# Fetching half of the search stretches from SP instead of GpSimd in a graph attention kernel

## The reference

```python
h = x @ w_lin + b_lin                       # x: (12500, 64)
msg = h[edge_src]                           # 400,000 edges, sorted by edge_dst
counts = segment_sum(ones, edge_dst)        # edges of each node
pos = arange(e) - starts[edge_dst]
dense[edge_dst, pos] = msg                  # (12500, 32, 64), edges past the 32nd are dropped
mask[edge_dst, pos] = True
xb = mab(dense, dense, enc weights, mask)   # attention among a node's up to 32 messages
xp = relu(xb @ pma_lin_w + pma_lin_b)
p  = mab(seed, xp, pma weights, mask)       # one learned query per node
dd = mab(p, p, dec weights)
out = layernorm(x + relu(dd))
```

## Time and profile before

| | |
|---|---|
| Median of 3 runs | 4168.89 us |
| The profiled execution: time / span | 4176.05 / 4174.2 us |
| PE busy | 3126.7 us (75%) |
| DVE busy | 3035.1 us (73%) |
| POOL busy | 3067.2 us (73%) |
| ACT busy | 1659.8 us (40%) |
| DMA | 88 GB/s over the span |
| TensorE's granted clock | 0.912 of full speed, mean |

### The profile page before, as it was taken

How to read it: one execution, slowest core, us unless ns; L and a number is a source line. 1 busy time by engine, 2 the same in 40 slices (tenths; PEclk the granted TensorE clock), 3 DMA queues, 4 the chain that set the end, 5 groups by cost and what they waited for, 6 DMA issues and landing times.

```text
span 4174.2 us, 87208 instructions
## 1 busy us (share of the span) xinstructions
PE 3126.7 (75%) x30724; PEld 2000.1 (48%) x30724; DVE 3035.1 (73%) x7088; ACT 1659.8 (40%) x2990; POOL 3067.2 (73%) x3236
## 2 busy tenths in 40 slices
PE   5677777777777777777777777777777777777776
PEld 3444444454444444444444454444444444444444
DVE  4677777777777777777777777777776777777876
ACT  2343443444434434443444343443443444434443
POOL 3777777777777777777777777777777777777772
PEclk7898999999999999999999999999999999999998
DMA  5333333333333333333333333333333333333331
GB/s 197 87 85 88 85 88 84 87 88 85 87 86 87 85 88 85 87 85 88 85 87 86 87 85 88 85 87 85 88 87 85 88 85 87 85 88 85 97 95 35
DMA packets 170668, 368.55 MB, mean 88 GB/s; under 512 B 56190, under 2 KB 109094, under 8 KB 170230
## 3 DMA queue, kind: packets, MB, share of 16 engines
q0 software_dynamic: 158032, 342.73, 30.7%
q1 hardware_dynamic: 11877, 19.76, 1.3%
q10 hardware_dynamic: 320, 0.10, 0.0%
HBM read 349.58 MB, written 16.32 MB: 88 GB/s over the span
## 4 chain that ended last, share of the span: by engine, by line
POOL 63%; issue 21%; PE 7%; DMA 4%; DVE 3%; POOLq 1%; ACT 0%; SPq 0%; ACTq 0%; DVEq 0%
POOL gathered L547 61%; DMA gathered<-node_table,idx 4%; POOL windows L510 2%; PE ps L724 2%; PE ps L651 2%; PE ps L697 2%; DVE xb L1119 1%; PE ps L639 1%; DVE probs_diag L1193 0%; DVE flags L908 0%; POOLq L122 0%; PE ps L606 0%; POOLq L124 0%; PE ps L752 0%; DVE h L1075 0%
## 5 line engine op out<-in xcount | busy, mean ns | idle before, releaser
L547 POOL DMA_INDIRECT gathered<-node_table,idx x3125 | 2969.4, 950 | 952.4 <-issue 934.4
L639 PE MATMUL ps<-ident,gathered 128*128 128x128 f32 x3128 | 608.0, 326 | 748.7 <-DMA gathered<-node_table,idx 748.4
L639 PEld LDWEIGHTS ps<-ident,gathered 128*128 128x128 f32 x3128 | 501.7, 204 | 1104.8 <-issue 1062.8
L803 ACT ACTIVATE qT<-ps,cols 128x512 f32<-128x512 f32 x391 | 268.9, 688 | 1238.8 <-PE ps L639 1237.8
L1119 DVE SCALAR_TENSOR_TENSOR xb<-ps,cols,h 128x512 f32<-128x512 f32 x391 | 292.6, 748 | 640.6 <-PE ps L697 640.0
L761 ACT ACTIVATE h_apart<-ps 64x512 f32<-64x512 f32 x782 | 462.8, 592 | 443.7 <-PE ps L639 434.1
L1193 DVE STREAM_TRANSPOSE probs_diag<-probs 32x512 f32<-32x512 f32 x784 | 549.0, 700 | 18.3
L697 PE MATMUL ps<-h,ff_diag 128*128 128x512 f32 x782 | 505.6, 734 | 29.8 <-DVE h L1075 29.7
L651 PE MATMUL ps<-probs_diag,gathered 128*64 128x128 f32 x6256 | 449.4, 287 | 79.0 <-issue 78.6
L651 PEld LDWEIGHTS ps<-probs_diag,gathered 128*64 128x64 f32 x6256 | 363.3, 167 | 247.4 <-issue 230.9
L724 PE MATMUL ps<-xb,pma_diag 128*128 128x512 f32 x782 | 454.4, 664 | 31.3 <-DVE xb L1119 26.9
(11 more groups left out here) (195 smaller groups left out, 3369.3 us busy)
## 6 DMA issues: line engine op xcount, KB each, us to landing
gathered<-node_table,idx POOLq DMA_INDIRECT x3125
node_table<-gathered SPq DMA_DIRECT2D x24, 384.0 KB, 2.8
out_rows<-rows SPq DMA_DIRECT2D x5, 416.0 KB
win_table<-in_dst SPq DMA_DIRECT2D x1, 1716.0 KB
win_table<-in_src SPq DMA_DIRECT2D x1, 1716.0 KB
windows<-win_table,win_idx POOLq DMA_INDIRECT x94, 3.7
rows<-in_x SPq DMA_DIRECT2D x2, 640.0 KB, 5.2
rows<-in_x SPq DMA_DIRECT2D x1, 768.0 KB, 7.2
```

Of the source, the lines that this page charges most:

```text
L547: pool.indirect_dma_start(out=gathered[:, s.slot(0, RING), t * ROW:(t + 1) * ROW], out_offset=None, in_=table, in_offset=bass.IndirectOffs ...
L639: mm = pe.transpose(ps[:, bank, p * P:(p + 1) * P], gathered[:, s.slot(0, RING), lo:lo + 2 * ROW - 2:3], ident[:, :])
L803: nc.scalar.activation(qT[:, s.slot(0, 4), :], ps[:, B_Q, :], ACT.Identity, bias=c_("q_b", P)).then_inc(q_sb, 1)
```

## The change

SP takes over the stretches of every second group (the odd ones, from group 5 on). DVE still writes the 128 row numbers into `win_idx`; for an odd group it then transposes them in blocks of 32 (`odd_turned`), so that partitions 0, 32, 64 and 96 each hold 32 of them in one row. SP waits for that, and four times loads 32 numbers into registers and issues 32 DMAs, each of one row of `win_table` (704 int32) to one partition. The SP loop has 23 rounds of two groups, and one more group stands behind it: 47 groups, 6016 row DMAs. `windows` has three buffers: 0 for the even groups, 1 and 2 for the odd ones in turn. DVE waits for four semaphores, one per 32 rows, where the group is odd. POOL's `gather_windows` is called for even groups only. To make room in SBUF, `consts` is half as wide, `ones` borrows `pool_part`, and the compare results in `flags`, which nobody reads, are BF16.

```diff
+DIRECT_BUFFER = (0, 1, 0, 2)
...
-        flags = [sb(f"flags{i}", [P, n]) for i, n in enumerate((SAMPLES, WIN, WIN))]
+        ones = pool_part[0:SAMPLE_ROWS, 0:P]
+        flags = [sb(f"flags{i}", [P, n], BF16) for i, n in enumerate((SAMPLES, WIN, WIN))]
+        odd_turned = sb("odd_turned", [P, 2, DEG], I32)
-        windows = sb("windows", [P, 2, 2 * WIN + DEG], I32)
+        windows = sb("windows", [P, 3, 2 * WIN + DEG], I32)
...
+            def odd_rows(b, count):
+                wait_apart(sp, odd_turned_ready, count, sp_passed)
+                for q in range(QUADS):
+                    _, at = nc.values_load_multi_w_load_instructions(
+                        odd_turned[DEG * q:DEG * q + 1, b, :], engines=(mybir.EngineType.SP,), min_val=0,
+                        max_val=SAMPLES - 1, skip_runtime_bounds_check_because="a count of the samples, less one")
+                    for j in range(DEG):
+                        sp.dma_start(windows[DEG * q + j:DEG * q + j + 1, 1 + b, 0:2 * WIN],
+                                     win_table[bass.ds(at[j], 1), :]).then_inc(odd_in[b][q], 16)
+            sp.wait_ge(table_in, 64)
+            with sp.Fori(0, (ITS - 6) // 4) as pair:
+                odd_rows(0, pair * 2 + 1)
+                odd_rows(1, pair * 2 + 2)
+            odd_rows(0, ITS // 2 - 2)
...
-                if s.has_iteration(AT_STRETCH) and (s.looped or s.at >= 16 + AT_STRETCH):
+                if s.has_iteration(AT_STRETCH) and s.slot(AT_STRETCH, RING) == 0 and (s.looped or s.at >= 16 + AT_STRETCH):
...
-                V.tensor_scalar(win_idx[:, at:at + 1], win_row[:, at:at + 1], -1.0, None, ALU.add).then_inc(win_idx_ready, 1)
+                minus = V.tensor_scalar(win_idx[:, at:at + 1], win_row[:, at:at + 1], -1.0, None, ALU.add)
+                if at % 2 == 0:
+                    minus.then_inc(win_idx_ready, 1)
+                else:
+                    n = s.round(AT_ROWS) - 1
+                    minus.then_inc(odd_idx_ok, 1)
+                    wait_apart(dve, odd_idx_ok, n, dve_passed)
+                    V.transpose(odd_turned[:, at // 2, :], win_idx[:, at:at + 1].broadcast_to((P, DEG))
+                                ).then_inc(odd_turned_ready, 1)
...
+                at = s.slot(AT_SEARCH, PERIOD) // OCTS_PER_IT
+                if at % 2:
+                    for q in range(QUADS):
+                        dve.wait_ge(odd_in[at // 2][q], s.period(AT_SEARCH) * (16 * DEG))
+                    return 1 + at // 2
```

More of the change, by code:

```diff
@@ L96, in round, with period @@
         return self.group * (PERIOD // RING) + (self.at - lag) // RING
+    def period(self, lag):
+        return self.group + (self.at - lag) // PERIOD
     def slot(self, lag, n):
@@ L313, in gnn_kernel @@
         x_in = [sem(f"x_in{i}") for i in range(6)]
-        win_in = [sem(f"win_in{i}") for i in range(2)]
+        win_in = [sem(f"win_in{i}") for i in range(3)]
+        odd_in = [[sem(f"odd_in{b}{q}") for q in range(QUADS)] for b in range(2)]
+        odd_idx_ok = sem("odd_idx_ok")
+        odd_turned_ready = sem("odd_turned_ready")
         found = sem("found")
@@ L507, in _, with gather_windows @@
             one_where_zero(ident[:, :], [[-1, P]], 0)
-            def gather_windows(u, buffer, at):
-                wait_apart(pool, win_idx_ready, u - (DIRECT - 1), pool_passed)
+            def gather_windows(s):
+                wait_apart(pool, win_idx_ready, s.round(AT_STRETCH) - 1, pool_passed)
+                at = s.slot(AT_STRETCH, PERIOD) // OCTS_PER_IT
                 pool.indirect_dma_start(
-                    out=windows[:, buffer, 0:2 * WIN], out_offset=None, in_=win_table,
-                    in_offset=bass.IndirectOffsetOnAxis(ap=win_idx[:, at:at + 1], axis=0)).then_inc(win_in[buffer], 16)
+                    out=windows[:, 0, 0:2 * WIN], out_offset=None, in_=win_table,
+                    in_offset=bass.IndirectOffsetOnAxis(ap=win_idx[:, at:at + 1], axis=0)).then_inc(win_in[0], 16)
             def gather_direct(u):
@@ L517, in gather_direct @@
                     pool.indirect_dma_start(
-                        out=windows[:, u % 2, c * WIN:(c + 1) * WIN], out_offset=None,
+                        out=windows[:, DIRECT_BUFFER[u], c * WIN:(c + 1) * WIN], out_offset=None,
                         in_=edges.rearrange("(n o) -> n o", o=1),
-                        in_offset=bass.IndirectOffsetOnAxis(ap=win_elem[:, u:u + 1], axis=0)).then_inc(win_in[u % 2], 16)
+                        in_offset=bass.IndirectOffsetOnAxis(ap=win_elem[:, u:u + 1], axis=0)).then_inc(win_in[DIRECT_BUFFER[u]], 16)
             for u in range(2):
@@ L539, in step @@
                         pool.wait_ge(table_in, 64)
-                    at = s.slot(AT_STRETCH, PERIOD) // OCTS_PER_IT
-                    gather_windows(s.iteration(AT_STRETCH), at % 2, at)
+                    gather_windows(s)
                 wait_apart(pool, av_ps, s.octet(RING - 1), pool_passed)
@@ L577, in _ @@
                 hi = min(lo + 512, SAMPLES)
-                pe.matmul(ps_samples[:, lo:hi], ones[:, :], flat[:, lo:hi], start=True, stop=True
+                pe.matmul(ps_samples[:, lo:hi], ones, flat[:, lo:hi], start=True, stop=True
                           ).then_inc(samples_ps, 1)
@@ L910, in count_rows, with rows_of @@
                 dve.wait_ge(sampled, count)
-            def rows_of(u, at):
+            def rows_of(s):
+                u = s.iteration(AT_ROWS)
+                at = s.slot(AT_ROWS, PERIOD) // OCTS_PER_IT
                 count_rows(u, at, u + 1)
-                V.tensor_scalar(win_idx[:, at:at + 1], win_row[:, at:at + 1], -1.0, None, ALU.add).then_inc(win_idx_ready, 1)
+                minus = V.tensor_scalar(win_idx[:, at:at + 1], win_row[:, at:at + 1], -1.0, None, ALU.add)
[7 more added lines that the diff above has]
+                                ).then_inc(odd_turned_ready, 1)
             def elements_of(u):
@@ L924, in elements_of, with direct_landed, landed @@
                                 ).then_inc(win_elem_ready, 1)
-            def landed(u, half):
-                direct = 2 if not isinstance(half, int) else min(half + 1, 2)
-                dve.wait_ge(win_in[u], half * 16 + (16 + 16 * direct))
+            def direct_landed(u):
+                b = DIRECT_BUFFER[u]
+                dve.wait_ge(win_in[b], 32 * DIRECT_BUFFER[0:u + 1].count(b))
+            def landed(s):
+                u = s.iteration(AT_SEARCH)
+                if not s.looped and u < DIRECT:
+                    direct_landed(u)
+                    return DIRECT_BUFFER[u]
+                at = s.slot(AT_SEARCH, PERIOD) // OCTS_PER_IT
[3 more added lines that the diff above has]
+                    return 1 + at // 2
+                dve.wait_ge(win_in[0], s.round(AT_SEARCH) * 16 + (32 * DIRECT_BUFFER.count(0) - 16))
+                return 0
             def search(u, h, buffer, at):
@@ L1036, in _ @@
             iota_slots = iota_j[:, :].unsqueeze(1).broadcast_to((P, 2, DEG))
+            searched = [0]
             def step(s):
@@ L1176, in step @@
                     par = s.slot(AT_SEARCH, RING) // OCTS_PER_IT
-                    landed(par, s.round(AT_SEARCH))
-                    count_edges(u, par, par)
-                    shift(u, par, range(BITS - 1, SHIFTS - 1, -1))
+                    searched[0] = landed(s)
+                    count_edges(u, par, searched[0])
+                    shift(u, searched[0], range(BITS - 1, SHIFTS - 1, -1))
                 if s.has_iteration(AT_SHIFT) and (s.looped or s.at >= 8 + AT_SHIFT):
-                    par = s.slot(AT_SHIFT, RING) // OCTS_PER_IT
-                    shift(s.iteration(AT_SHIFT), par, range(SHIFTS - 1, -1, -1))
+                    shift(s.iteration(AT_SHIFT), searched[0], range(SHIFTS - 1, -1, -1))
                     for lag in (12, 11, 10, 9):
@@ L1185, in step @@
                             dve.wait_ge(g_in[s.slot(lag, RING)], s.round(lag) * (16 * OCT) + 16 * OCT)
-                    index_of(par, s.slot(AT_SHIFT, PERIOD) // OCTS_PER_IT)
+                    index_of(searched[0], s.slot(AT_SHIFT, PERIOD) // OCTS_PER_IT)
                 if s.has_iteration(AT_ROWS) and (s.looped or s.at >= 4 * DIRECT + AT_ROWS):
-                    rows_of(s.iteration(AT_ROWS), s.slot(AT_ROWS, PERIOD) // OCTS_PER_IT)
+                    rows_of(s)
             def to_diagonal(s, pr, first, last):
```

10 lines of the change are left out of this document (5 added, 5 removed).

## The result

The changed kernel takes 4109.51 us (median of 4 runs, 4106.90 to 4112.06) where the kernel before, run beside it on the same chip, takes 4168.64 (4 runs, 4167.66 to 4169.90). The ratio is 0.9858, with a 95% interval of 0.9841 to 0.9875: faster by 59.1 us, 1.4%. The forecast was 4110.

A forecast was written before the change was run, and what follows sets the result against it. The prediction took POOL's number of indirect DMAs as the bound. Removing 47 fetches at 1.251 us takes 58.8 us off the median, 4168.89 - 58.8 = 4110.1, with all added work hidden; forecast 4110, range 4100 to 4160.

The forecast's parts named there:

- The bound: POOL's queue: its number of indirect DMAs sets the pace from first gather to last, at 4108.43 us.
- The gain: On POOL: 47 of the 94 stretch fetches leave, each 1.251 us on the path, 58.8 us in all.
- What is late next: POOL again, with one fetch in 65 indirect DMAs; two groups take 81.4 us where they took 82.9.
- SP's row: On SP: issue and register arithmetic of one row DMA, 0.53 us taken, 0.38 to 0.64; 128 rows are 68 us.
- The loads: On SP: four loads of 32 registers per group, 5 us in all, range 0.1 to 15.
- The pass: SP's work on one group, rows and loads: 73 us, ends 49 and 97, has to be under 81.4.
- The rival of a slow SP: SP's pass exceeds 81.4 us, so DVE waits at odd searches and POOL then for indices: 4784 us, chance 0.13.
- its formula: Loss in us from an SP pass of T: 46 x (T - 81.4) + (T - 84.0) - 23.8.
- T: SP's pass time over one group in the slow-SP case; 96.3 us there, with the whole gain eaten at 83.2.
- The other rivals: PE and DVE nearer the bound, 4140, chance 0.04; BF16 count slowing gathers, 4185, 0.02; POOL still waiting, 4169, 0.01.
- The BF16 result: On DVE: sample count with BF16 results might slow gathers beside it, 75 us back, 4185; chance 0.02.
- SP's stores: On SP: result stores, starting at 3919 us before, queue behind its last pass to about 4000, covered by POOL's end.

The follow-up runs named there:

- Three of four: Changed kernel, but SP fetches 70 of the 94 groups, with byte offsets from DVE and four `windows` buffers: 4080.49 us, ratio 0.9791 to the kernel before.
- sixteen loads: Changed kernel, but SP loads its 32 registers 16 times per group instead of 4: 4484.44 us, ratio 1.0737 to the kernel before.

## Why the prediction was right

- **The bound.** Right. The chain after is the same queue, and putting the 47 fetches back took all of the gain (ratio 0.9998). Three of four, with 70 fetches gone, gained 87.7 us for 87.6.
- **The gain.** 47 x 1.251 = 58.8 us was forecast; medians differ by 59.1, POOL's own groups by 58.9.
- **What is late next.** POOL again, with rounds of two groups of about 81.3 to 81.4 us.
- **SP's row.** 0.53 us was taken, of 0.38 to 0.64; it is 0.417, near the low end. The DMA itself takes 0.225, less than the 0.33 that I held to be its least: a lone issue in the earlier trace rows is of another shape, and no lower bound for this one. The fused instruction takes 0.037, and a move of 0.029 comes with it that I had counted neither in the prediction nor in the section on the change. The sum of the three, 0.291, is less than the 0.417 between rows; what fills the rest isn't in the profile.
- **The loads.** 5 us for four was taken, of 0.1 to 15; it is 8.5. I took one short instruction per register, 0.04 us; a register costs 2.12 / 32 = 0.066. The range had little behind it, and that 8.5 lay inside is in part luck. The Trainium skill's figure (Runtime: NRT & Kernel Launch, Instruction fetch mechanics) of about 200 ns a register would make 6.4 us of each load. The trace has 188 of them, between 2.04 and 2.19 us. Here the measurement decides: a third of the page's figure, which would have turned the sign.
- **The pass.** 73 us forecast, 61.9 found. Row and load were off in opposite directions, 14 and 3.5 us. The slack is not 8 but 18 us a round. Either miss alone would still have left the pass under 81.4 (76.5 with the loads as found, 58.4 with the row).
- **The rival of a slow SP** did not come about, but its formula held: 378 us by the measured pass for sixteen loads, where 4484.4 is 375 above the changed kernel's 4109.5. Its weak point was T, not the price. The chance of 0.13 was fair to what the rows of before could say, and larger than the measured slack would ask for.
- **The other rivals.** POOL's waits for PE shrank, from 18.0 to 9.7 us, so PE and DVE were not near. The BF16 result left the count at 1.51 us, and the gathers at 0.949. SP's stores did queue behind its last pass, as forecast: the first goes out at 3943.2, behind the last row of 3942.9. It cost nothing; the stores after it waited for DVE, up to 121.3 us, and the last at 4105.1 is behind POOL's last gather.
- **What the prediction did not see.** All of it was said of a chip on which POOL sets the pace. On two others POOL doesn't, and on the one of them where the changed kernel was run beside the kernel before it lost 0.3%. No row of before could tell this, as they are all of one chip.

## What to carry to other kernels

When one queue never waits, its instruction count is the time: price the instruction from start to start, multiply, and move what another idle sequencer can do. Ask of the new place two things, a throughput and a latency, and bound them from rows; here a pass that fitted cost nothing, and one that missed cost its excess in every round. And test such a change where the bound is that queue: with another bound the same edit can lose. When you idle an engine to price its work, look whether the others still do the same work: a DMA share of 44% for 19% said here that they did not.

## What the runs showed of the hardware

- A load of 32 registers from SBUF took 2.12 us, 0.066 per register. A row DMA with its address from a register occupied SP for 0.225 us, and rows came 0.41 us apart (0.42 in the mean) with the address arithmetic, and some 0.09 less without it. On the chip at 6400.62 the pass of the same instructions was 113.7 us for 62.0, with the same median durations and the same 0.41 in the median.
- 6016 such one-row DMAs brought 2 packets each into the hardware queue (11877 to 23909 in all) and raised its share only from 1.3 to 2.8% of the engines' time.
- With gathers that read one single row of the table in half of the groups, the gathers' queue took up 66.4% of the DMA engines for the same bytes, where real indices took 30.0%; on the other two chips 43.0 and 44.1% for some 19%. The kernel with such gathers and an idle SP was still within 9 us of the changed one.
- The same program took 4109 us on one chip and 6419 on another, with nearly the same busy time on POOL, DVE and ACT. Most of the difference stands as PE's idle time between small matmuls of about 0.22 us (1739.3 of 2304 us), and its cause stays open.
